# Four layers of graph attention: signed and scaled minimum, copies on ACT in the first layer, relu ahead of the fills in the second

## The reference

```
layer 0: scores = (h Wq)(h Wk)^T / 8; masked by adj; softmax; times (h Wv)
layer 1: four heads with biases; scores -> leaky_relu(0.2) -> + mask -> softmax -> times values;
         mean over heads, leaky_relu
layer 2: e_ij = sum_f a_f * leaky_relu(u_if + v_jf); masked softmax; times hp; elu
layer 3: e_ij = leaky_relu(src_i + dst_j); masked softmax; times Wh; + h W_res; elu; layernorm, gamma, beta
```

## Time and profile before

| | |
|---|---|
| median of 3 runs | 3784.64 us (3781.56 to 3786.26) |
| the profiled execution | 3785.15 us, span of its core 3783.4 us |
| busy, share of the span | PE 84%, DVE 86%, ACT 78%, POOL 27% |
| layer 0, units | about 33 to 320 us |
| layer 1, units | about 355 to 1380 us |
| layer 2, units | about 1455 to 3370 us |
| layer 3, units | about 3405 to 3783 us |

### The profile page before, as it was taken

One profiled execution on the slowest core, in us unless ns is written; L12 is line 12 of the kernel. 1 busy time (PEld: TensorE's weight loads), 2 busy tenths in 40 slices (PEclk: granted clock), 3 DMA queues, 4 the chain that ended last, 5 costly groups with the idle time before them and its releaser, 6 DMA issues. The chain is left out here.

```text
span 3783.4 us, 80082 instructions
## 1 busy us (share of the span) xinstructions
PE 3194.2 (84%) x31515; PEld 1745.3 (46%) x31515; DVE 3269.9 (86%) x5325; ACT 2960.2 (78%) x3529; POOL 1014.7 (27%) x565
## 2 busy tenths in 40 slices
PE   6886988998999878889898898888988978878786
PEld 4663666665666643333333333333333323336665
DVE  7885887887888779999999999999999999966666
ACT  4554877887788758989899899888998889956555
POOL 4332555555555630000000001000000000016554
PEclk9997999999999989999999999999999999988887
DMA  6551000000000000000000000000000000001111
GB/s 180 172 183 38 18 17 17 18 18 19 18 18 15 21 13 7 10 12 10 10 10 10 10 10 10 10 10 10 11 12 10 10 10 10 10 14 52 49 51 43
DMA packets 67260, 110.69 MB, mean 29 GB/s; under 512 B 25941, under 2 KB 25944, under 8 KB 66904
## 3 DMA queue, kind: packets, MB, share of 16 engines
q1 hardware_dynamic: 66904, 105.77, 9.4%
HBM read 86.87 MB, written 18.87 MB: 28 GB/s over the span
## 5 line engine op out<-in xcount | busy, mean ns | idle before, releaser
L975 ACT ACTIVATE l_scalar_ring<-l_w,l_r 128x1024 f32<-128x1024 f32 x1600 | 1679.8, 1143 | 35.7 <-DVE l_values L1021 26.1
L1089 DVE TENSOR_SCALAR l_vector_ring<-l_w_code,l_r_code 128x2048 f32<-128x2048 f32 x1248 | 1619.2, 1362 | 3.5 <-issue 0.2
L922 PE MATMUL scores<-l_vector_ring,l_signs_code 128*32 128x512 f16 x9984 | 686.4, 396 | 194.8 <-DVE l_vector_ring L1089 193.7
L912 PE MATMUL scores<-l_scalar_ring,l_signs 128*32 128x512 f32 x6400 | 781.3, 607 | 67.7 <-ACT l_scalar_ring L975 66.7
L239 ACT COPY probs_t<-turned 128x512 f32<-128x512 f32 x512 | 293.4, 586 | 494.7 <-PE turned L198 491.5
L434 POOL TENSOR_TENSOR l_masked<-l_relu,mask 128x1024 f32<-128x1024 f32 x256 | 545.5, 2131 | 493.8 <-ACT l_relu L582 491.2
L922 PEld LDWEIGHTS scores<-l_vector_ring,l_signs_code 128*32 128x32 bf16 x9984 | 240.0, 96 | 669.8 <-DVE l_vector_ring L1089 399.2
L209 PE MATMUL outT<-probs_t,l_values 128*64 128x128 f32 x6144 | 436.6, 285 | 66.0 <-ACT probs_t L239 26.3
L198 PE MATMUL turned<-ident,l_probs 128*128 128x128 f32 x3072 | 437.7, 288 | 11.4 <-issue 7.3
L209 PEld LDWEIGHTS outT<-probs_t,l_values 128*64 128x64 f32 x6144 | 345.1, 140 | 214.6 <-DVE l_acc L665 102.4
L269 ACT ACTIVATE l_probs<-l_logits,negmax,l_bound 128x1024 f32<-128x1024 f32 x320 | 397.6, 1242 | 6.8 <-DVE negmax L260 6.8
(11 more groups left out here) (244 smaller groups left out, 3331.8 us busy)
## 6 DMA issues: line engine op xcount, KB each, us to landing
mask<-masks_kept SPq DMA_DIRECT2D x192, 256.0 KB, 2.6
l_adj<-adj SPq DMA_DIRECT2D x64, 512.0 KB, 4.4
masks_kept<-mask SPq DMA_DIRECT2D x64, 256.0 KB, 2.3
x_res<-x SPq DMA_DIRECT2D x8, 256.0 KB, 5.0
out<-x_res SPq DMA_DIRECT2D x8, 256.0 KB, 3.5
l_w_both<-L_gnn_Wq SPq DMA_DIRECT2D x2, 64.0 KB
l_w_both<-L_gnn_Wk SPq DMA_DIRECT2D x2, 64.0 KB
l_w_both<-L_gnn_Wv SPq DMA_DIRECT2D x2, 64.0 KB
```

The source lines that it names most:

```text
L912: last = nc.tensor.matmul(s.scores[g * ROWS:(g + 1) * ROWS, buf, half, :], signs[:, window], scalar_ring[:, at % SCALAR_RING, g, halves[ha ...
L922: last = nc.tensor.matmul(s.scores[g * ROWS:(g + 1) * ROWS, buf, half, :], signs_code[:, par, g % 2, window], parts(vector_ring[:, at % VE ...
L975: last = nc.scalar.activation(scalar_ring[:, at % SCALAR_RING, g, :], w[:, par, :], ACT.Relu, bias=r[:, par, column:column + 1])
L1089: last = nc.vector.tensor_scalar(vector_ring[:, at % VECTOR_RING, g:g + 2, :], w_code[:, par, :, :], r_code[:, par, 0, column:column + 1], ...
```

## The change

1. `masked_max`: one operation `(scores + mask) * minus_scale` with the minimum over the row, written straight to `negmax`. The drain and the second operation are gone, the logits are stored with the sign turned and scaled, and `exponentials` has the constant scale -1. This is in all four layers.
2. Layer 0: ACT copies both halves of `turned`, DVE none. Four loads of `adj` are under way instead of two, the masks have eight slots of their own, and POOL makes them six units ahead.
3. Layer norm: centring and squaring on POOL are two steps; centring goes from unit 1 to 2 (layer 1) or 3 (layer 0), squaring to unit 4, applying from 6 to 12 (layer 1) or 7 (layer 0). DVE's scale reduction goes from unit 2 to 8 (layer 1) or 5 (layer 0). Layers 2 and 3 keep their places.
4. Layer 1: ACT's relu stands ahead of the fill's high part instead of behind it.

The diff, without the hunks of layers 2 and 3, where only calls follow the new arguments:

```diff
--- before.py
+++ after.py
@@ -88,7 +88,6 @@
         self.turned_out = sb("turned_out", [P, P], F32)
         self.ident = sb("ident", [P, P], F32)
         self.add_halves = sb("add_halves", [P, D], F32)
-        self.rowmax = sb("rowmax", [P, 4], F32)
         self.negmax = sb("negmax", [P, 4], F32)
         self.rowsum = sb("rowsum", [P, 4], F32)
         self.rinv = sb("rinv", [P, 4], F32)
@@ -147,8 +146,12 @@
     wait(g, sems["y_ready"], done)
     nc.gpsimd.tensor_tensor(s.centred[:], s.graph(b), s.stat[:, 1, :].unsqueeze(2).to_broadcast(shape),
                             ALU.subtract).then_inc(sems["centred_ready"], 1)
+
+
+def layer_norm_square(g, s, sems, done):
+
     g.wait_ge(sems["centred_ready"], done + 1)
-    nc.gpsimd.tensor_tensor(s.square[:], s.centred[:], s.centred[:], ALU.mult).then_inc(sems["square_ready"], 1)
+    s.nc.gpsimd.tensor_tensor(s.square[:], s.centred[:], s.centred[:], ALU.mult).then_inc(sems["square_ready"], 1)
 
 
 def variance(v, s, stat, total):
@@ -251,22 +254,19 @@
     sp.dma_start(s.mask[:, slot, :], s.kept_mask(m)).then_inc(sems[f"mask_in{slot}"], 16)
 
 
-def masked_max(v, s, sems, logits, slot, bias_scale, out, mask):
+def masked_max(v, s, sems, logits, slot, minus_scale, out, mask):
 
     hold_waits(v, sems)
-    s.nc.vector.tensor_tensor_reduce(out=out, in0=logits, in1=mask, scale=1.0, scalar=-3e38, op0=ALU.add,
-                                     op1=ALU.max, accum_out=s.rowmax[:, slot:slot + 1])
-    v.drain()
-    s.nc.vector.tensor_scalar(s.negmax[:, slot:slot + 1], s.rowmax[:, slot:slot + 1], bias_scale, None,
-                              ALU.mult).then_inc(sems["logits_ready"], 1)
-
-
-def exponentials(a, s, sems, logits, probs, slot, u, scale, buffers=2, summed=True):
+    s.nc.vector.tensor_tensor_reduce(out=out, in0=logits, in1=mask, scale=minus_scale, scalar=3e38, op0=ALU.add,
+                                     op1=ALU.min, accum_out=s.negmax[:, slot:slot + 1]).then_inc(sems["logits_ready"], 1)
+
+
+def exponentials(a, s, sems, logits, probs, slot, u, buffers=2, summed=True):
 
     a.wait_ge(sems["logits_ready"], STARTS + u + 1)
     wait(a, sems["turned_ready"], STARTS + u + 1 - buffers)
     total = s.rowsum[:, slot:slot + 1] if summed else None
-    s.nc.scalar.activation(probs, logits, ACT.Exp, bias=s.negmax[:, slot:slot + 1], scale=scale, accum_out=total
+    s.nc.scalar.activation(probs, logits, ACT.Exp, bias=s.negmax[:, slot:slot + 1], scale=-1.0, accum_out=total
                            ).then_inc(sems["probs_ready"], 1)
 
 
@@ -308,14 +308,15 @@
     PIECES = 2
     WIDTH = s.N // PIECES
     K = 2 + PIECES * QK + H
-    LOADS = 2
-    AHEAD = 3
+    LOADS = 4
+    SLOTS = NB
+    AHEAD = 6
     with ExitStack() as ctx:
         def sb(name, shape, dt):
             return ctx.enter_context(nc.sbuf_tensor(f"{layer}_{name}", shape, dt))
 
-        sems = make_sems(nc, ctx, layer, ["mask_kept0", "mask_kept1", "mask_kept2", "mask_kept3", "x_in0", "x_in1", "x_in", "relu_ready", "masked_ready", "bound_ready", "zeros_ready"]
-                         + [f"adj_in{i}" for i in range(LOADS)])
+        sems = make_sems(nc, ctx, layer, ["x_in0", "x_in1", "x_in", "relu_ready", "masked_ready", "bound_ready", "zeros_ready"]
+                         + [f"adj_in{i}" for i in range(LOADS)] + [f"mask_kept{i}" for i in range(SLOTS)])
 
         w_in = sb("w_in", [P, 3, H, D], F32)
         w_both = sb("w_both", [P, 3, H, D], F32)
@@ -342,7 +343,8 @@
         masked = sb("masked", [P, 2, N], F32) if leaky else None
         acc = sb("acc", [P, D], F32)
         leaked = sb("leaked", [P, D], F32)
-        adj32 = sb("adj32", [P, 2, N], I32) if adj_dram is not None else None
+        adj32 = sb("adj32", [P, LOADS, N], I32) if adj_dram is not None else None
+        mask_ring = sb("mask_ring", [P, SLOTS, N], BF16) if adj_dram is not None else None
         exp_scale, neg_scale = bound[:, 20:21], bound[:, 21:22]
         least, power, inverse, scales, w_scales, v_back = (bound[:, 3 * i:3 * i + 3] for i in range(6))
         unit_out = s.outT[:, P:P + D]
@@ -393,22 +395,19 @@
 
                 def keep_mask(m, slot):
                     sp.wait_ge(sems["mask_ready"], m + 1)
-                    sp.dma_start(s.kept_mask(m), s.mask[:, slot, :]).then_inc(sems[f"mask_kept{slot}"], 16)
+                    sp.dma_start(s.kept_mask(m), mask_ring[:, slot, :]).then_inc(sems[f"mask_kept{slot}"], 16)
 
                 for i in range(LOADS):
                     load(i, i)
                 for b in range(2, B):
                     load_x(b, "x_in")
-                for m in range(LOADS, MASK_SLOTS):
-                    keep_mask(m - LOADS, m - LOADS)
+                for m in range(LOADS, B * NB):
+                    keep_mask(m - LOADS, (m - LOADS) % SLOTS)
                     load(m, m % LOADS)
-                for m in range(MASK_SLOTS, B * NB):
-                    keep_mask(m - LOADS, (m - LOADS) % MASK_SLOTS)
-                    load(m, m % LOADS)
-                for i in range(LOADS):
-                    keep_mask(B * NB - LOADS + i, (i - LOADS) % MASK_SLOTS)
-                for slot in range(MASK_SLOTS):
-                    sp.wait_ge(sems[f"mask_kept{slot}"], 16 * B * NB // MASK_SLOTS)
+                for m in range(B * NB - LOADS, B * NB):
+                    keep_mask(m, m % SLOTS)
+                for slot in range(SLOTS):
+                    sp.wait_ge(sems[f"mask_kept{slot}"], 16 * B)
             else:
                 for m in range(B * NB):
                     wait(sp, sems["masked_ready"], (m - 1) * H)
@@ -416,13 +415,13 @@
 
         @block.gpsimd
         def _(g):
-            def mask(four, i):
-
-                g.wait_ge(sems[f"adj_in{i % LOADS}"], 16 * (four * (MASK_SLOTS // LOADS) + i // LOADS) + 16)
-                wait(g, sems[f"mask_kept{i}"], 16 * four)
-                wait(g, sems["logits_ready"], STARTS + MASK_SLOTS * four + i + 1 - MASK_SLOTS)
+            def mask(b, i):
+
+                g.wait_ge(sems[f"adj_in{i % LOADS}"], 16 * (b * (SLOTS // LOADS) + i // LOADS) + 16)
+                wait(g, sems[f"mask_kept{i}"], 16 * b)
+                wait(g, sems["logits_ready"], STARTS + SLOTS * b + i + 1 - SLOTS)
                 hold_waits(g, sems)
-                nc.gpsimd.tensor_scalar(s.mask[:, i, :], adj32[:, i % LOADS, :], -MASKED, MASKED, ALU.mult, ALU.add
+                nc.gpsimd.tensor_scalar(mask_ring[:, i, :], adj32[:, i % LOADS, :], -MASKED, MASKED, ALU.mult, ALU.add
                                         ).then_inc(sems["mask_ready"], 1)
 
             def mask_relu(pair, i, n, u):
@@ -438,23 +437,27 @@
 
 
                 for n in range(U):
-                    if n == 1:
+                    if n == (2 if leaky else 3):
                         layer_norm_centre(g, s, sems, next_norm(s, b), b + 2)
-                    if n == 6:
+                    if n == 4:
+                        layer_norm_square(g, s, sems, b + 2)
+                    if n == (12 if leaky else 7):
                         layer_norm_apply(g, s, sems, next_norm(s, b), par, b + 2, b * K + 2)
                     if leaky and not (last_graph and n + 3 >= U):
                         i = ((n + 3) // H) % NB
                         mask_relu((b + (n + 3) // U) * (NB // 2) + i // 2, i % 2, n + 3, b * U + n + 3)
                     if not leaky and not (last_graph and n + AHEAD >= NB):
-                        mask(b * (NB // MASK_SLOTS) + (n + AHEAD) // MASK_SLOTS, (n + AHEAD) % MASK_SLOTS)
+                        mask(b + (n + AHEAD) // SLOTS, (n + AHEAD) % SLOTS)
 
             if leaky:
                 for u in range(3):
                     mask_relu(0, 0, u, u)
             else:
                 layer_norm_centre(g, s, sems, 0, 0)
+                layer_norm_square(g, s, sems, 0)
                 layer_norm_apply(g, s, sems, 0, 0, 0, 0)
                 layer_norm_centre(g, s, sems, 1, 1)
+                layer_norm_square(g, s, sems, 1)
                 mask(0, 0)
                 layer_norm_apply(g, s, sems, 1, 1, 1, 0)
                 for i in range(1, AHEAD):
@@ -585,16 +588,15 @@
             def graph(b, par, project, last_graph):
                 for n in range(U):
                     u = b * U + n
+                    if not leaky:
+                        copy_half(a, nc.scalar.copy, s, sems, 0, u)
                     copy_half(a, nc.scalar.copy, s, sems, 1, u)
                     if not (last_graph and n + 1 == U):
                         exponentials(a, s, sems, logits[:, (n + 1) % 2, :], probs[:, (n + 1) % 2, :],
-                                     (n + 1) % 4, u + 1, exp_scale)
-                    fills = steps_fills(n, project)
-                    for k in fills[:1]:
-                        high_part(b + 1, 1 - par, k)
+                                     (n + 1) % 4, u + 1)
                     if leaky and not (last_graph and n + 3 >= U):
                         relu(n + 3, u + 3)
```

(16 more changed lines are left out.)

5 lines of the change are left out of this document (3 added, 2 removed).

## The result

The changed kernel takes 3681.55 us (median of 4 runs, 3667.0 to 3683.27) against 3784.84 us: 103 us less, a ratio of 0.9726 (95% interval 0.9711 to 0.974). The forecast was 3702 us, 83 less, in a range of 3655 to 3755. The profiled execution took 3681.38 us, its span 3679.5.

The account below looks back on a forecast made before the run. DVE was taken to bound the additive layer, loops of waits layers 0 and 1. Savings 22 + 45 + 10 + 6 = 83 us gave 3785 - 83 = 3702 us, range 3655 to 3755.

Parts of the forecast that it names:

- the four terms: Savings forecast by layer: layer 0 22 us, layer 1 45, additive layer 2 10, last layer 3 6.
- The operation with a scale from a tile: One-operation maximum on DVE: tile scale adds 0.06 us in layers 0 and 1, nothing elsewhere; 1.28 and 1.22 us.
- The rival in which it is slow: All layers: the one operation takes 1.7 instead of 1.22 us, making the kernel slower, 3834 us; chance 0.06.
- DVE's time for the removed step: DVE's queue, all layers: 0.21 us saved per operation, or 0.15 where the operation takes 154 ns; accumulator read stays.
- Layer 0: plain units 3.44 to 3.39, unit 2 from 5.60 to 3.5, unit 4 by 0.4, the graph's end by 0.5: Layer 0: 3.1 us less per graph in 7 graphs, 22 us; bounds 12 and 27.
- Layer 0: loads and slots, 0: Layer 0: four loads and eight mask slots save nothing, as DVE never waited for masks; possible cost 0 to 3 us.
- Layer 1, the step and relu: Layer 1: one-operation maximum and relu ahead of the fill save 48 us with other small terms, rounded to 45.
- the loop worked out: Layer 1 fill units: exponentials 1.16 to relu, 0.92 to fill copy, 0.68 for it; 7.4 us over two units.
- That rival: Layer 1: the fill copy takes relu's place as DVE's wait, layer 1 gives only 12, 3735 us; chance 0.20.
- Layer 1, the moved layer norm: 0, bounds -10 and +10: Layer 1: scale reduction from unit 2 to 8, also a fill unit and assumed blocked there too, is worth 0.
- Layer 2, 10, bounds 0 and 14: Additive layer: DVE is its bound, so 64 x 0.15 = 10 us saved; bounds 0 and 14.
- Layer 3, 6, bounds 0 and 13: Last layer: 64 x 0.17 = 11 us at most, half taken, 6, as DVE is only 66% busy.

Follow-up runs that it names:

- e1: Changed kernel with the old two-step maximum (drain, separate sign and scale operation) in all four layers, exponentials' scale from a tile in layers 0 and 1: 3728.71 us.
- e6: Changed kernel with layer 0's layer norm in its old places (centring and squaring unit 1, scale reduction unit 2, applying unit 6): 3680.98 us.
- e4: Changed kernel with half 0 of the transposed probabilities copied on DVE again in layer 0: 3674.95 us.
- e2: Kernel before the change with only the one-operation maximum with sign and scale, in all layers, and -1 as the exponentials' scale: 3712.05 us.
- e7: Changed kernel with two loads of adj under way instead of four, masks still six units ahead in eight slots: 3676.65 us.
- e3: Changed kernel with the fill's high part ahead of relu on ACT again in layer 1: 3702.39 us.
- e5: Changed kernel with layer 1's layer norm in its old places (centring and squaring unit 1, scale reduction unit 2, applying unit 6): 3697.11 us.
- e8: Changed kernel with the old two steps of the maximum in layer 3 alone: 3686.88 us.
- e10: Changed kernel with DVE's mean (unit 0) and scale reduction (unit 8) of layer 1 ahead of their unit's logits: 3680.18 us.

## Why the prediction was right, and where it was off

*Sign and direction.* Right, and each of the four terms had the right sign: 22, 45, 10, 6 forecast; 17.1, 52.2, 15.4, 21.2 measured.

*The operation with a scale from a tile.* Forecast 1.28 in layers 0 and 1 and 1.22 in the others: 1.28 and, in layer 2, 1.22 measured. In layer 3 it takes 1.52 on the mean, but it did so before too, so the change left it alone. The rival in which it is slow is gone.

*DVE's time for the removed step.* Mis-sized: I kept the accumulator read's 0.08 in DVE's queue. The next operation doesn't wait for it: here in layer 2, start to start,

```profile
2020.29 1.22 DVE L260 CUSTOM_DVE_ANT_0 l_logits<-scores,mask 128x1024 f32<-128x1024 f32 x1
2021.43 0.08 DVE L260 DVE_READ_ACCUMULATOR2_ANT negmax<- 128x1 f32 x1
2021.43 2.60 DVE L1093 TENSOR_SCALAR l_vector_ring<-l_w_code,l_r_code 128x2048 f32<-128x2048 f32 x2
```

where before it was this:

```profile
2003.53 1.22 DVE L257 CUSTOM_DVE_ANT_0 l_logits<-scores,mask 128x1024 f32<-128x1024 f32 x1
2004.67 0.08 DVE L257 DVE_READ_ACCUMULATOR2_ANT rowmax<- 128x1 f32 x1
2004.83 0.15 DVE L260 TENSOR_SCALAR negmax<-rowmax 128x1 f32<-128x1 f32 x1
2004.90 2.60 DVE L1089 TENSOR_SCALAR l_vector_ring<-l_w_code,l_r_code 128x2048 f32<-128x2048 f32 x2
```

1.37 has become 1.14: 0.23 a unit, not 0.15, and 64 x 0.23 = 15 us against 15.4 measured (and 15.3 back in e1). Of this, 0.16 is from the read's start to the small operation behind the drain, and 0.07 from there to the next operation: the drain goes too, which I hadn't counted there. In layer 1 the 0.06 of the tile's scale is paid out of 0.29, which leaves the 0.22 that the trace shows.

*Layer 0: plain units 3.44 to 3.39, unit 2 from 5.60 to 3.5, unit 4 by 0.4, the graph's end by 0.5.* The sizes hold: in the changed kernel the exponentials behind unit 4 start 5.15 apart (148.08 and 153.23) instead of 5.67,

```profile
148.08 1.16 ACT L269 ACTIVATE l_probs<-l_logits,negmax 128x1024 f32<-128x1024 f32 x1
...
151.40 0.69 ACT L578 ACTIVATE l_kh<-fill,l_qk_bias 128x512 f16<-128x512 f32 x1 [1.48 <-PE fill L489]
152.27 1.07 ACT L242 COPY probs_t<-turned 128x512 f32<-128x512 f32 x2 [0.18 <-PE turned L201]
153.23 1.17 ACT L269 ACTIVATE l_probs<-l_logits,negmax 128x1024 f32<-128x1024 f32 x1
```

but the whole is 17.1, not 22. I had taken the 5.60 for every graph: in the seven that project, the unit took 4.75 to 5.60 before, 5.39 on the mean, so its gain is 1.9 and not 2.1. A graph's end gives 0.3 on the mean and not 0.5, and a plain unit takes 3.48, where it took 3.44 and I forecast 3.39. The step that failed is the attribution. I put 2.1 us a graph down to the place of the scale reduction and nothing to the half copies. e6 and e4 show that either of the two is enough: with the copies on ACT the old place costs 2.1 us in the whole layer, with the new place the copies on DVE cost nothing, and with neither (e2) the layer is 8.7 longer. The interval behind unit 2 is 3.51 to 4.16 in e6, 3.56 to 3.69 in e4 and 4.52 to 5.39 in e2. By the order of the streams, both make DVE reach `copy_out` of unit 2 in time, and what is in time can't be made more so. I had also assumed that the operation on `stat` would be blocked at its new place as well: in layer 0 it takes 0.17 there in every graph, in layer 1 0.44 to 1.00.

*Layer 0: loads and slots, 0.* Right for the loads (e7).

*Layer 1, the step and relu.* Together 48 less 3 were forecast. Undone singly they cost 22.6 (e1) and 18.6 (e3), 41 in sum. The chain was right: relu stands 1.15 behind the exponentials instead of 1.81, the idle ahead of the logits is halved, and the low part starts 2.77 behind the exponentials (721.76 and 724.53), as in the loop worked out (1.16 + 0.92 + 0.68), after a new wait of 0.46. That rival exists as a mechanism, at the q fills, but did not take the gain.

*Layer 1, the moved layer norm: 0, bounds -10 and +10.* Wrong, beyond its bound: it is worth 17.3 us (e5). I had read two of its stalls and left them where they were because unit 8 is a fill unit like unit 2. What I missed is what lies next to it: in unit 2 the reduction comes right behind centring and squaring on POOL, two operations of 1.04 that push the masked sum of the following units back, and it then finds POOL in that sum. The two moves were not undone apart, but the intervals between the starts of the exponentials, summed over the eight graphs, show where e5 is longer than the changed kernel: 18.4 us between the exponentials of units 4 and 5, behind the old place of the scale reduction, less 7.2 between those of units 10 and 11, behind its new place; 10.3 between those of units 9 and 10, behind the old place of the applying, less 4 from 14 to 18, around its new one. That POOL and the scale reduction are what makes these units long is read from their places. On the other side, the early relu brings POOL's sum under the mean's small operation in unit 0. It takes 0.17 in seven of the eight graphs of e3 and 1.28 to 1.75 in six of the eight of the changed kernel, and the units behind it are 7.6 us longer in all than in e3. (The 3.79 us in the expectation of e5 is the unit ahead of that; before, the unit behind the mean took 3.95 to 4.11 in six of the graphs, 8.06 in the first and 6.76 in the last.) I had named no such cost. So 45 against 52.2 is in part luck: the step and the relu were forecast somewhat too high, and a term set to nothing was worth 17. Undone singly, the three add up to 58.5 us, more than the 52.2, so they overlap too.

*Layer 2, 10, bounds 0 and 14.* That DVE is the limit was right. The measured 15.4 lies beyond the upper bound; the term was mis-sized as above.

*Layer 3, 6, bounds 0 and 13.* 21.2, beyond the bound. The step itself is worth 11 to 12 (e8, e1): I took half of its 11 and should have taken the whole. The other 9 to 10 us stay open, but the one trace of before shows where they lie. Unit by unit, it and e8, which has the same two steps in this layer, differ in two graphs: by 6.8 us in the fourth and by 3.2 in the sixth (a unit of 7.13 against 4.07; the changed kernel's trace has one of 7.11 there as well). In the fourth graph one unit takes 13.63 us instead of 8.46, and in it DVE stands still twice without waiting for anything that the profile shows:

```profile
3544.97 0.17 DVE L1462 RECIPROCAL rinv<-rowsum 128x1 f32<-128x1 f32 x1 [2.69 <-issue]
3548.17 0.28 DVE L1465 SCALAR_TENSOR_TENSOR l_z<-scores,rinv,l_residual 128x64 f32<-128x64 f32 x1 [3.03 <-issue]
```

None of the other 13 traces has such a stall above 0.5 us in this layer. It is not simply one unlucky execution: the others of before are hardly shorter (medians of 3780.16 to 3784.84 against 3785.15 here). Whether they stall too, and what the stall is, is not shown. The length of this layer also scatters by 12 us between executions of the same code, and the granted clock of the stretch goes with it: 338.2 us at 0.84 (e3), 332.1 at 0.86, 326.1 at 0.88 (e4); which of the two sets the other is not shown.

## What to carry to other kernels

Where two edits relieve the same late engine, each looks worth the whole gain alone and nothing on top of the other: undo them singly and also together before a gain is put down to one. A small operation is priced by what it can be blocked by, not by its size: look at what the neighbour engine runs in that microsecond. Before a gain is split by layer from one trace each, learn how well each layer repeats, and go through the units one by one for a stall that only one trace has.

## What the runs showed of the hardware

A `TENSOR_SCALAR` on 128x8 in SBUF takes 0.17 us at the median and up to 2.13 (e10) beside POOL's masked sum of 2.13 us. In the traces of before, the changed kernel, e3, e5 and e10, wherever it takes over 0.25 us, it ends 0.02 to 0.03 us behind an instruction of POOL that was under way. This agrees with the Trainium skill, page SBUF: State Buffer, section "Who interferes with whom", by which a DVE tensor_scalar in a two-port mode and a GpSimd instruction exclude each other: the one that is issued first blocks the other until it has ended. That this operation runs in such a mode is not shown by itself. By the same section `TENSOR_REDUCE` is never blocked; its 0.67 to 0.69 in all 64 places of the changed kernel agrees, one of them (714.27) with POOL's masked sum under way.

With scores from PSUM the custom operation takes 1.22 us with a constant as scale and 1.28 with a 128x1 tile. The exponentials went the other way, from a tile to a constant, and take 1.155 on the mean instead of 1.242. The read of the accumulator (0.08 us) need not hold up DVE: the next operation can start together with it (both at 2021.43 above).
